# Attention over eight images: results kept with queries on partitions, and a second, turned copy of x

## What is computed

```python
# x: (8, 128, 32, 32); Wq, Wk: (64, 128); Wv: (128, 128); b is the image, c the channel, n = h*w = 1024 pixels
xf = x.reshape(b, c, n)
q = einsum('oc,bcn->bon', Wq, xf) + bq[None, :, None]
k = einsum('oc,bcn->bon', Wk, xf) + bk[None, :, None]
v = einsum('oc,bcn->bon', Wv, xf) + bv[None, :, None]
attn = softmax(einsum('bci,bcj->bij', q, k), axis=-1)
out = einsum('bcn,bmn->bcm', v, attn).reshape(b, c, h, w)
return gamma * out + x
```

## Time and profile before

| | |
|---|---|
| median of three runs | 235.01 us (235.0 to 235.23) |
| span of the profiled execution (first to last instruction) | 233.8 us |
| PE busy | 226.9 us, 97% |
| ACT busy | 179.6 us, 77% |
| POOL busy | 176.6 us, 76% |
| DVE busy | 164.3 us, 70% |
| share of the DMA engines | 33.8% for the queue that carries nearly all |
| granted PE clock | full, until the last slice |

### The profile page before, as it was taken

The page is one execution under the profiler, slowest core; times in us unless marked ns, Lnnn a source line. Parts: engine busy times, 40 slices in busy tenths (PEclk is TensorE's granted clock), DMA queues, the critical chain, the costliest instruction groups (busy, mean ns, idle before and its releaser), DMA issues.

```text
span 233.8 us, 4852 instructions
## 1 busy us (share of the span) xinstructions
PE 226.9 (97%) x1672; PEld 196.5 (84%) x1672; DVE 164.3 (70%) x289; ACT 179.6 (77%) x345; POOL 176.6 (76%) x158
## 2 busy tenths in 40 slices
PE   7997999999999999999999999999999999999994
PEld 5464988989889888898889898898888899899892
DVE  1587388776878777776878767687687767683455
ACT  2669787688887878689887888789786878778952
POOL 8687997299973898579983898658983977768770
PEclk9999999999999999999999999999999999999998
DMA  3556400670409322490407504291105801010102
GB/s 96 151 180 155 117 0 2 142 178 3 135 3 233 82 67 73 96 222 0 135 5 185 129 5 134 39 235 44 45 3 132 185 0 46 4 45 3 45 0 90
DMA packets 16871, 20.13 MB, mean 86 GB/s; under 512 B 9936, under 2 KB 10704, under 8 KB 16848
## 3 DMA queue, kind: packets, MB, share of 16 engines
q1 hardware_dynamic: 16400, 19.63, 33.8%
q10 hardware_dynamic: 448, 0.20, 0.3%
HBM read 4.33 MB, written 4.19 MB: 36 GB/s over the span
## 4 chain that ended last, share of the span: by engine, by line
PE 92%; DVE 3%; DMA 1%; ACT 1%; issue 1%; ACTq 0%; DVEq 0%
PE sums L600 26%; PE scores L581 13%; PE sums L616 13%; PE scores L582 12%; PE work L532 12%; PE work L526 6%; PE work L542 3%; DVE neg_max L829 2%; PE work L520 1%; PE work L519 1%; PE work L521 1%; DMA w_qk<-in_L_conv_Wk 1%; PE scores L642 1%; PE scores L526 1%; PE sums L515 1%
## 5 line engine op out<-in xcount | busy, mean ns | idle before, releaser
L456 POOL TENSOR_TENSOR weight_lo<-weight,weight_hi 128x512 bf16<-128x512 f32 x90 | 124.7, 1405 | 39.3 <-ACT weight_hi L763 38.8
L829 DVE TENSOR_REDUCE neg_max<-work 128x1 f32<-128x512 f32 x120 | 81.7, 686 | 28.4 <-PE work L532 28.2
L760 ACT ACTIVATE weight<-scores 128x512 f32<-128x512 f32 x128 | 76.9, 600 | 25.2 <-PE scores L582 21.3
L600 PEld LDWEIGHTS sums<-values,weight_hi 128*128 128x128 f32 x504 | 77.2, 188 | 10.4 <-issue 0.5
L600 PE MATMUL sums<-values,weight_hi 128*128 128x258 f32 x504 | 80.8, 282 | 0.1
L763 ACT ACTIVATE weight_hi<-scores 128x512 fp32r<-128x512 f32 x128 | 76.9, 601 | 0.0
L581 PE MATMUL scores<-q_hihi,k_hilo 128*128 128x512 f32 x128 | 54.5, 426 | 0.7 <-ACT weight_hi L763 0.7
L582 PE MATMUL scores<-q_lomax,k_hione 128*128 128x512 f32 x128 | 50.3, 393 | 0.0
L532 PE MATMUL work<-k_hilo,q_hihi 128*128 128x512 f32 x120 | 48.1, 405 | 0.7 <-DVE neg_max L829 0.3
L616 PE MATMUL sums<-values_b,weight_lo 128*128 128x130 bf16 x496 | 34.3, 221 | 0.0
L871 DVE TENSOR_TENSOR weight_lo<-weight,weight_hi 128x512 bf16<-128x512 f32 x38 | 31.8, 838 | 2.7 <-ACT weight_hi L763 2.7
(11 more groups left out here) (84 smaller groups left out, 173.5 us busy)
## 6 DMA issues: line engine op xcount, KB each, us to landing
out<-y_sb SPq DMA_DIRECT2D x15, 256.0 KB, 2.4
x_sb<-in_x SPq DMA_DIRECT2D x7, 512.0 KB, 3.8
q_hihi<-qk_hi SPq DMA_DIRECT2D x12, 256.0 KB, 4.4
q_lomax<-qk_lo SPq DMA_DIRECT2D x7, 256.0 KB, 5.0
k_hione<-qk_hi SPq DMA_DIRECT2D x7, 256.0 KB, 4.9
k_hilo<-qk_hi SPq DMA_DIRECT2D x6, 256.0 KB, 3.1
k_hilo<-qk_lo SPq DMA_DIRECT2D x6, 256.0 KB, 5.0
q_lomax<-neg_max_r SPq DMA_DIRECT2D x56, 0.5 KB, 2.1
```

The lines of the kernel that those rows point to most:

```text
L456: pool.tensor_tensor(weight_lo[:, r], weight[:, r], weight_hi[:, r], ALU.subtract).then_inc(weight_lo_pool_done, 1)
L600: last = pe.matmul(sums[:, it, 0:VCOLS], weight_hi[:, r, tile(it)], values[p][:, j], start=(j == 0), stop=False)
L760: act.activation(weight[:, r], scores[:, s % 2], ACT.Exp)
L829: dve.reduce_max(neg_max[:, t, h:h + 1], place, AX.X, negate=True).then_inc(neg_max_done, 1)
```

## The change

The output array gets the shape (8, 128, 8, 128): image, pixel within a tile, tile, channel. The host gives the kernel a second copy of x in that layout (`x_turned`) and brings the output back to the layout of the reference. So nothing has to be turned on PE.

- `out` jobs, `turn_out`, `turn_last`, POOL's `scale` and the buffer `scaled` go.
- SP loads `x_turned`, 512 KB an image, into a ring of three buffers. The bias is now needed along the free dimension, so `b_v` is loaded with 128 copies and `gamma_bv` is 128x128.
- POOL adds the bias to the loaded `x_turned` in place (`add_bias`, k = 7 and 11).
- DVE's `finish` is now four instructions, one per tile of 128 queries: `total` times `one_over` (a value per partition) plus `x_turned`. All of its operands are in SBUF. It stands at k = 2 and 10, one step after `add_half`; the old one stood at k = 7 and 15 in DVE's program.
- For the last chunk DVE does the scaling as before and then a `tensor_tensor` instead of turn and add.

```diff
+TURNED = 3
@@ side_jobs
-    if k == 6 and b > 0:
-        jobs.append(("out", 2 * b - 1, 0))
-    if k == 14:
-        jobs.append(("out", 2 * b, 0))
...
-        b_v = sbuf("b_v", [CHANNELS, 1], fp32)
+        b_v = sbuf("b_v", [128, CHANNELS], fp32)
-        gamma_bv = sbuf("gamma_bv", [128, 1], fp32)
+        gamma_bv = sbuf("gamma_bv", [128, CHANNELS], fp32)
+        x_turned_sb = sbuf("x_turned_sb", [TILE, TURNED, TILES, CHANNELS], fp32)
...
@@ SP
+            def load_x_turned(n):
+
+                wait(sp, y_done, CHUNK_TILES * HALVES * (n - TURNED + 1))
+                sp.dma_start(x_turned_sb[:, n % TURNED], x_turned[n]).then_inc(x_turned_loaded[n % TURNED], 16)
...
             def store_y(c):
-                sp.wait_ge(y_done, c + 1)
+                sp.wait_ge(y_done, CHUNK_TILES * (c + 1))
...
             spread_by_halves()
+            for n in range(2):
+                load_x_turned(n)
             for b in range(BATCHES):
                 if b > 0:
                     send_max_row(2 * b + 1)
                     store_y(2 * b - 1)
                     if b + IMAGES - 1 < BATCHES:
                         load_x(b + IMAGES - 1)
+                    if b + 1 < BATCHES:
+                        load_x_turned(b + 1)
@@ POOL
-            def scale(c):
...
+            def add_bias(c):
+
+                n, h = divmod(c, HALVES)
+                pool.wait_ge(x_turned_loaded[n % TURNED], 16 * (n // TURNED + 1))
+                place = x_turned_sb[:, n % TURNED, quarter(h)]
+                bias = gamma_bv[:, :].rearrange("p (a c) -> p a c", a=1).broadcast_to([TILE, CHUNK_TILES, CHANNELS])
+                pool.tensor_tensor(place, place, bias, ALU.add).then_inc(with_bias_done, 1)
...
-                if k == 3 and b > 0:
-                    scale(2 * b - 1)
-                if k == 11:
-                    scale(2 * b)
+                if k in (7, 11):
+                    add_bias(2 * b + (7, 11).index(k))
@@ DVE
-            def finish(c, place):
...
+            def finish(c):
+
+                n, h = divmod(c, HALVES)
+                dve.wait_ge(with_bias_done, c + 1)
+                dve.wait_ge(one_over_done, c + 1)
+
+                wait(dve, y_stored[h], 16 * n)
+                for it in range(CHUNK_TILES):
+                    dve.scalar_tensor_tensor(y_sb[:, h, it], total[:, it, 0:CHANNELS], one_over[:, it:it + 1],
+                                             x_turned_sb[:, n % TURNED, h * CHUNK_TILES + it],
+                                             ALU.mult, ALU.add).then_inc(y_done, 1)
...
+                if s >= TILES + LAG and (s - LAG) % TILES == 0:
+                    finish((s - LAG) // TILES - 1)
```

More of the change, by code:

```diff
@@ L124, in wait, with attention_program @@
         engine.wait_ge(semaphore, count)
-def attention_program(nc, x, Wq, bq, Wk, bk, Wv, bv, gamma, out):
+def attention_program(nc, x, x_turned, Wq, bq, Wk, bk, Wv, bv, gamma, out):
     fp32 = mybir.dt.float32
@@ L200, in attention_program @@
         x_loaded = [sem(f"x_loaded{i}") for i in range(IMAGES)]
+        x_turned_loaded = [sem(f"x_turned_loaded{i}") for i in range(TURNED)]
         spread_mx = [sem(f"spread_mx{p}") for p in range(2)]
@@ L311, in wait_lo_summed @@
                 engine.wait_ge(burst_done, s // TILES + 1)
-        def last_place(it):
-            return scores[:, it] if it < 2 else bank(it - 2)
         def store_last(engine, it):
-            engine.wait_ge(y_done, CHUNKS + it)
-            engine.dma_start(out_dram[BATCHES - 1][:, chunk(1)][:, tile(it)], y_sb[:, 1, tile(it)]).then_inc(last_stored, 16)
+            engine.wait_ge(y_done, CHUNK_TILES * (CHUNKS - 1) + it + 1)
+            engine.dma_start(out[BATCHES - 1][:, CHUNK_TILES + it], y_sb[:, 1, it]).then_inc(last_stored, 16)
         @block.sync
@@ L363, in store_y @@
             def store_y(c):
-                sp.wait_ge(y_done, c + 1)
-                sp.dma_start(out_dram[c // HALVES][:, chunk(c % HALVES)], y_sb[:, c % HALVES]).then_inc(y_stored[c % HALVES], 16)
+                sp.wait_ge(y_done, CHUNK_TILES * (c + 1))
+                sp.dma_start(out[c // HALVES][:, quarter(c % HALVES)], y_sb[:, c % HALVES]).then_inc(y_stored[c % HALVES], 16)
             sp.dma_start(x_sb[:, 0, chunk(0)], x_dram[0][:, chunk(0)]).then_inc(first_x_loaded[0], 16)
@@ L375, in _ @@
             sp.dma_start(w_v[:, :], Wv).then_inc(rest_loaded, 16)
-            sp.dma_start(b_v[:, :], bv.rearrange("(p a) -> p a", a=1)).then_inc(rest_loaded, 16)
+            sp.dma_start(b_v[:, :], bv.rearrange("(a c) -> a c", a=1).broadcast_to([128, CHANNELS])).then_inc(rest_loaded, 16)
             sp.dma_start(gamma_col[:, :], gamma.rearrange("(p a) -> p a", a=1).broadcast_to([128, 1])).then_inc(rest_loaded, 16)
@@ L538, in turn_max @@
                 last.then_inc(mt_done, 1)
[L540 to L547, removed]
             def do_max(c, i):
@@ L568, in do_job @@
                     turn_max(n, place)
-                elif name == "out":
-                    pe.wait_ge(scaled_done, n + 1)
-                    turn_out(range(CHUNK_TILES), place)
             def score_tile(s):
@@ L707, in _ @@
                 last.then_inc(sums_done, 1)
[L708 to L711, removed]
         @block.scalar
@@ L863, in do_job @@
                     rest_of_v(n, i, bank(bank_of(job)))
-                elif name == "out":
-                    finish(n, bank(bank_of(job)))
             def low_weights(s):
@@ L876, in add_half @@
                 if half == 0:
-                    wait(dve, scaled_done, c)
+                    wait(dve, y_done, CHUNK_TILES * c)
                 dve.tensor_tensor(total[:, its], sums[:, its, CHANNELS:2 * CHANNELS + 1], low_sum[:, its],
@@ L951, in scale_last @@
                 dve.wait_ge(one_over_done, c + it + 1)
-                dve.scalar_tensor_tensor(scaled[:, it], sums[:, it, CHANNELS:2 * CHANNELS], one_over[:, it:it + 1],
+                dve.scalar_tensor_tensor(total[:, it, 0:CHANNELS], sums[:, it, CHANNELS:2 * CHANNELS], one_over[:, it:it + 1],
                                          low_sum[:, it, 0:CHANNELS], ALU.mult, ALU.add).then_inc(last_scaled, 1)
             def finish_last(it):
-                dve.wait_ge(out_turned, c + it + 1)
-                dve.scalar_tensor_tensor(y_sb[:, h, tile(it)], last_place(it)[:, tile(it)], gamma_bv[:, :],
-                                         image(n)[:, chunk(h)][:, tile(it)], ALU.add, ALU.add).then_inc(y_done, 1)
+                dve.wait_ge(last_scaled, it + 1)
+                dve.tensor_tensor(y_sb[:, h, it], total[:, it, 0:CHANNELS], x_turned_sb[:, n % TURNED, h * CHUNK_TILES + it],
+                                  ALU.add).then_inc(y_done, 1)
             invert_last(0)
@@ L984 @@
     arrays, args = {}, []
-    for name in _INS:
-        a = np.ascontiguousarray(inputs[name])
+    given = {name: inputs[name] for name in _INS}
+    tiled = np.asarray(inputs["x"]).reshape(BATCHES, CHANNELS, TILES, TILE)
+    given["x_turned"] = tiled.transpose(0, 3, 2, 1)
+    for name in ["x", "x_turned"] + _INS[1:]:
+        a = np.ascontiguousarray(given[name])
         arrays[f"in_{name}"] = a
@@ L991 @@
     result = run_bass_kernel_spmd(nc, [arrays], core_ids=[0])
-    return result.results[0]["out_0"]
+    made = result.results[0]["out_0"]
+    return np.ascontiguousarray(made.transpose(0, 3, 2, 1)).reshape(BATCHES, CHANNELS, 32, 32)
```

26 lines of the change are left out of this document (8 added, 18 removed).

## The result

| | before | after |
|---|---|---|
| median | 235.0 us | 258.8 us (257.8 to 259.0, four runs) |
| ratio to before | | 1.098 (95% interval 1.093 to 1.102) |
| span of the profiled execution | 233.8 us | 257.0 us |

A forecast was written before the change was run, and what follows sets the result against it. PE, busy 97% of the span, was taken as the bound. Waits of 20.2 us less 6.7 us saved gave +13.5 on span 233.8, so 247.3, and 248.5 us as time; range 230.0 to 252.

The forecast's parts named there:

- Turns removed: On PE's path, 15 `out` jobs of 0.44 us each go: 6.6 us off.
- The end: Last four tiles: the turn and hand-over go, but DVE still needs 3.0 to 3.4 us; 0.1 us off.
- Two SBUF inputs against POOL: DVE's new `finish` at k = 10: it and POOL exclude each other for whole instructions; the four end at 123.05 from 119.3.
- the two bounds: DVE's four: either it keeps its turn (1.15 us and one wait), or POOL gets in each time; the second was taken.
- The overlap of 70 ns: DVE's records overlap by some 70 ns, so 0.27 to 0.28 us start to start and 1.15 us for the four.
- The rival in which DVE keeps its turn: At k = 10 DVE runs all four through, or POOL is slow to get in: 231.1 us, chance 0.20.
- PE's waits: PE waits for late DVE: 2.9 us in images 1 to 5, 2.8 in 6, 2.1 in 0, 0.8 in 7.
- `add_bias` at k = 7 as a cause: On POOL, which runs without a gap there, `add_bias` (taken as 1.15 us) pushes all behind it back.
- The sum: All images: waits 20.2 us later, 6.7 us sooner, +13.5 on span 233.8, so 247.3.
- From span to time: Whole run: runs lie 1.2 us above the span, taking 247.3 to 248.5 us.
- Transfers: x_turned loads, 512 KB an image, 3.8 us as for x: hidden unless early or late by over ten microseconds.
- The range: Whole kernel: 230.0 to 252 us, reaching to the faster side, leaving out most of no-collision and the upper tail.

The follow-up runs named there:

- e11_bias3: Changed kernel with POOL's add_bias of an image's first chunk at k = 3 instead of k = 7; 284.2 us (ratio 1.206).
- e1_fill: Changed kernel with nine extra unused 128x128 matmuls on PE before the job that waits for DVE, in images 0 to 6; 250.4 us (ratio 1.062).
- e6_before_wait6: Kernel before the change, with DVE reducing mx(10) six times more in images 1 to 6, results unused; 263.6 us (ratio 1.119).
- e5_one_input: Changed kernel with x left out of y: four tensor_scalar a chunk with one SBUF input each; 252.4 us (ratio 1.076).
- e4_two: Changed kernel with y made by two 128x512 instructions a chunk instead of four of 128x128, same places; 243.7 us (ratio 1.035).
- e7_before_wait4: Kernel before the change, with DVE reducing mx(10) four times more in images 1 to 6, results unused; 246.5 us (ratio 1.048).

## Why the prediction was right in its mechanism and wrong in its time

- **Turns removed, 6.6 us.** Right as far as can be seen: where the rest is out of the way, 5.3 to 6.0 us are gained in all.
- **The end, 0.1 us.** Too small: from the second inversion to the last y DVE took 3.23 us before (228.44 to 231.67) and 2.78 after (252.07 to 254.85), where 3.0 to 3.4 had been added up. That is 0.3 us more off than forecast.
- **Two SBUF inputs against POOL, and POOL gets in each time.** Right, and the choice between the two bounds, drawn from the earlier trace rows, held: 3.52 us for the four (worked out: 3.75), 4.10 in image 6 (4.2), 5.33 in image 7 (4.8), 1.14 at k = 2 (1.15). The overlap of 70 ns behind the 1.15 was read from the wrong pair, as the two reductions of the earlier trace rows start 0.68 apart; the value held all the same. The rival in which DVE keeps its turn needed 1.15 us and one wait at k = 10.
- **PE's waits.** 2.48 in images 1 to 5 (2.9), 2.6 in image 6 (2.8), 3.27 in image 0 (2.1 taken of 2.1 to 3.3), 0.9 at the end (0.8): 19.2 in all against 20.2.
- **`add_bias` at k = 7 as a cause.** Wrong in emphasis: with it at k = 3 instead (e11_bias3, k = 10) the four take longer, not shorter. Its place matters for what it keeps free.
- **The term that was missing.** This is the step that failed. The sum priced "it waits some 2.9 us" with 2.9 us, so it took PE's speed behind the wait as given. In the trace of before the clock was at full until the last slice, and no PE wait there exceeded 1.5 us, so it had no row for what a longer wait does. Each of the seven waits but one was followed by 3.41 us at the lower level, 1.7 us each, 10.2 in all. 247.3 of forecast span less 1 for the waits plus 10.2 gives 256.5 against 257.0. That is nearly the whole distance between 248.5 and 258.8; filling the waits (e1_fill) gave back 8.4 us of it.
- **From span to time.** The forecast added 1.2 us to a span to get a time, as the difference of a median and the span of another run. Within one run the time lies 1.8 us above the span, with the changed kernel (258.8 and 257.0) as with the one before (235.6 and 233.8). So 0.6 us of the 10.3 between forecast and time are of this conversion.
- **Transfers.** x_turned lands in 5.2 us instead of the 3.8 that x showed, x itself in 4.5, and nothing waited for either.
- **The range.** Its upper end, 252, was drawn from the lengths of the waits alone. The bound should have held what the engine does after a wait that the kernel before never had.

## What to carry to other kernels

Before putting short VectorE instructions that need GpSimd's way to SBUF (two SBUF inputs, or a tensor_scalar from SBUF to SBUF) in front of a result that TensorE waits for, look at what GpSimd does at that place in the timeline: price each of them behind the first with one whole GpSimd instruction, or put them where GpSimd is idle. Fewer, longer ones cost less there, but no run had them for nothing (1.8 us against 3.5 where a short GpSimd instruction stood between, 3.2 to 3.4 against 4.0 to 4.1 beside long ones). And when a change gives TensorE a wait that it never had, count the slower clock behind it: here a wait of 1.55 us cost 1.9 on average, and one of 2.7 cost 4.7.

## What the runs showed of the hardware that I had not expected

- With PE waits of 2.5 to 3.3 us the granted clock went to 0.50 for 3.41 us (once 6.83 in e6_before_wait6), mostly from 0.4 to 1.5 us after the wait's end, when PE worked without a break: 6 of 7 waits in the changed kernel, 6 of 6 in e6_before_wait6. It was 3 of 7 at 1.9 to 2.4 us in e5_one_input, 3 of 6 at 2.2 us in e11_bias3, 3 of 3 at 1.8 to 2.5 us in e4_two, none of 6 at 1.55 us in e7_before_wait4. So the length of a wait alone doesn't tell whether a fall comes.
- Nine matmuls of no use, 2.2 us of PE time in each wait, made the changed kernel 8.4 us faster.
- A tensor_scalar with one SBUF input takes turns with GpSimd like an instruction with two; a reduction from SBUF doesn't.
